# A graph layer's main path written out without loops, with 24 row buffers in turn, on one Trainium2 core

## The reference, cut to what matters

```python
h = jnp.maximum(_layernorm(x, axis=-1), 0.0)
hx = jnp.einsum('ni,rio->rno', h, weight)         # 8 x 12500 x 256
msg = hx[edge_type, src]
agg = jax.ops.segment_sum(msg, dst, num_segments=12500)
out = x + agg * 0.5 ** 0.5 + h_bias + (h @ loop_weight) * 0.5 ** 0.5
```

## Time and profile before

| what | value |
|---|---|
| median of 3 runs | 2342.75 us |
| the profiled execution, first to last instruction | 2975.6 us |
| instructions recorded | 39409 |
| first gather starts | 146.6 us |
| GpSimd's 1661 gathers, busy | 1631.7 us |
| TensorE busy (products of sums, of weights) | 1792.1 us (747.5, 1176.8) |
| VectorE busy | 1201.0 us |

### The profile page before, as it was taken

How to read it: one execution, slowest core, us unless ns; L and a number is a source line. 1 busy time by engine, 2 the same in 40 slices (tenths; PEclk the granted TensorE clock), 3 DMA queues, 4 the chain that set the end, 5 groups by cost and what they waited for, 6 DMA issues and landing times.

```text
span 2975.6 us, 39409 instructions
## 1 busy us (share of the span) xinstructions
PE 1792.1 (60%) x10566; PEld 1293.5 (43%) x10566; DVE 1201.0 (40%) x2675; ACT 520.9 (18%) x590; POOL 1699.8 (57%) x1687
## 2 busy tenths in 40 slices
PE   0046665665666666666675665666666665755667
PEld 0024444454444444444454444444444444443445
DVE  9834333343344343333343333333443334333433
ACT  4401111111111111111111111111111111111111
POOL 5466556565565565556555556466566555565553
PEclk9997777777777777777777767777777777777778
DMA  6533323333333333333333323233333333333232
GB/s 221 180 119 97 86 79 104 90 94 92 90 93 94 95 94 92 87 91 96 88 94 89 92 80 100 76 97 97 89 99 96 86 92 93 89 97 88 81 89 64
DMA packets 128701, 287.90 MB, mean 97 GB/s; under 512 B 31806, under 2 KB 71738, under 8 KB 125614
## 3 DMA queue, kind: packets, MB, share of 16 engines
q0 software_dynamic: 79728, 217.82, 26.0%
q1 hardware_dynamic: 47122, 57.12, 5.9%
q10 hardware_dynamic: 1836, 12.80, 1.0%
HBM read 262.01 MB, written 25.60 MB: 97 GB/s over the span
## 4 chain that ended last, share of the span: by engine, by line
PE 46%; issue 26%; DVE 12%; another core or an unknown queue 10%; DVEq 4%; DMA 1%; POOL 1%; ACT 0%; POOLq 0%; ACTq 0%; SPq 0%
PE ps_out L789 31%; PE sums L815 14%; DVE ring L683 4%; DVE onehot L641 2%; DVEq L672 2%; DVE result L662 1%; DVE stats L546 1%; DVE ring L652 1%; POOL rows L370 1%; PE ps_out L794 1%; DVEq L683 1%; DVE mv L563 1%; DMA rows<-h_table,index_now 1%; DMA xg<-x 0%
## 5 line engine op out<-in xcount | busy, mean ns | idle before, releaser
L370 POOL DMA_INDIRECT rows<-h_table,index_now x1661 | 1631.7, 982 | 1179.3 <-PE sums L815 531.0
L683 DVE TENSOR_TENSOR ring<-ring,sums 128x256 f32 x1661 | 700.3, 422 | 1715.5 <-remote 915.8
L789 PE MATMUL ps_out<-w_sb,stage 128*128 128x256 f32 x3072 | 1176.8, 503 | 208.7 <-issue 199.8
L815 PE MATMUL sums<-onehot,rows 128*128 128x128 f16 x6644 | 747.5, 245 | 869.5 <-issue 569.1
L815 PEld LDWEIGHTS sums<-onehot,rows 128*128 128x128 f16 x6644 | 526.0, 110 | 1189.6 <-issue 828.1
L789 PEld LDWEIGHTS ps_out<-w_sb,stage 128*128 128x128 f32 x3072 | 698.1, 250 | 378.0 <-issue 309.3
L452 ACT COPY index_now<-src_i 128x8 int32 (+1 forms) x196 | 38.8, 198 | 2128.0 <-PE sums L815 1687.0
L641 DVE TENSOR_TENSOR onehot<-lane,slot 128x768 f16<-128x768 f16 (+1 forms) x293 | 270.7, 924 | 0.4 <-issue 0.4
L459 ACT COPY stage<-ring 128x2048 f32 (+1 forms) x96 | 182.2, 1898 | 227.2 <-DVE carry L654 147.8
L462 ACT COPY ring<-zeros 128x2304 f32 (+1 forms) x96 | 202.8, 2112 | 10.9
L794 PE MATMUL ps_out<-w_sb,own_hT 128*128 128x256 f32 x384 | 112.6, 419 | 0.0
(11 more groups left out here) (52 smaller groups left out, 244.0 us busy)
## 6 DMA issues: line engine op xcount, KB each, us to landing
rows<-h_table,index_now POOLq DMA_INDIRECT x1661
own<-h_table SPq DMA_DIRECT2D x97, 128.0 KB
own_x<-x SPq DMA_DIRECT2D x97, 128.0 KB
out<-result SPq DMA_DIRECT2D x97, 128.0 KB
xg<-x SPq DMA_DIRECT2D x12, 1024.0 KB, 6.1
h_table<-tg ACTq DMA_DIRECT2D x12, 1024.0 KB, 8.2
w_sb<-weight SPq DMA_DIRECT2D x2, 1024.0 KB
dst_i<-dst SPq DMA_DIRECT2D x1, 833.0 KB, 10.5
```

The lines of the kernel that those rows point to most:

```text
L370: nc.gpsimd.indirect_dma_start(out=rows[:, k, :], out_offset=None, in_=table[:, :], in_offset=bass.IndirectOffsetOnAxis(ap=index_now[:, k: ...
L683: nc.vector.tensor_tensor(window, window, sum_of(k).rearrange("p (a w) -> p a w", w=W), ALU.add).then_inc(added, 1)
L789: nc.tensor.matmul(ps_out[:, 0:D], stage[:, m, :], w_sb[:, h, r, :], start=(m == 0), stop=False)
L815: last = nc.tensor.matmul(sum_of(k)[:, h * P:(h + 1) * P], rows[:, k, part * D + h * P:part * D + (h + 1) * P], onehot[:, k, :], start=(pa ...
```

## The change

All four compute engines and SP run the main path as straight code: every step, every wait value and every address is a constant. Further:
- GpSimd reads a chunk's indices from `src_i` itself; the copies by ScalarE and the waits on them are gone. `rows` has 24 buffers used in turn, with one wait for every four gathers.
- The ring is four tiles of 128 columns one behind the other and 16 columns behind the last. Only a window at the ring's end spills; `merge_spill` adds it to the ring's head and zeroes it once in four steps. `carry_tile` is gone. A window's offset is the node modulo 512, one VectorE piece in the head.
- `own`, `own_x` and `result` have two buffers each. `finish_tile` of a tile now comes after the second add of the next step.
- The 18 products of a tile are spread over the chunks from k = 5 on.
- The last two tiles are multiplied from the ring, with no copy, each in its own PSUM tensor; their own-row products go first.

```diff
-            def gather_step(s, count):
-                for k in range(count):
-                    for g, (a, b) in enumerate(INDEX_GROUPS):
-                        if k == a:
-                            pool.wait_ge(index_ready, len(INDEX_GROUPS) * s + g + 1)
-                    for a, b in BUFFER_GROUPS:
-                        if k == a:
-                            if not isinstance(s, int) or s > 0:
-                                pool.wait_ge(summed, K * (s - 1) + b)
-                            pass_gate(pool, pool_passed)
-                    nc.gpsimd.indirect_dma_start(
-                        out=rows[:, k, :], out_offset=None, in_=table[:, :],
-                        in_offset=bass.IndirectOffsetOnAxis(ap=index_now[:, k:k + 1], axis=0),
-                    ).then_inc(landed[k], 16)
+            def gather(c):
+                if c >= NB and c % NB_STEP == 0:
+                    pool.wait_ge(summed, c - NB + NB_STEP)
+                nc.gpsimd.indirect_dma_start(
+                    out=rows[:, c % NB, :], out_offset=None, in_=table[:, :],
+                    in_offset=bass.IndirectOffsetOnAxis(ap=src_i[:, c:c + 1], axis=0),
+                ).then_inc(landed[c % NB], 16)
...
-                gather_step(0, K)
-                with pool.Fori(1, STEPS - 1) as s:
-                    gather_step(s, K)
-                gather_step(STEPS - 1, K_LAST)
+                pool.wait_ge(s_src, 16)
+                for c in range(E_CHUNKS):
+                    gather(c)
...
             def stage_tile(t):
-                act.wait_ge(carried, t + 1)
+                act.wait_ge(added, chunks_before(t + 2))
+                if t % RING == 0:
+                    act.wait_ge(merged, spills_before(t + 1))
...
-                nc.vector.scalar_tensor_tensor(
-                    offsets[:, :, 0:K], tile_of.rearrange("p (s k) -> p s k", k=K), float(SLOT),
-                    within.rearrange("p (s k) -> p s k", k=K), ALU.mult, ALU.add).then_inc(s_window, 1)
+                nc.vector.tensor_scalar(offsets[:, :, 0:K], base_i[0:1, :].rearrange("p (s k) -> p s k", k=K),
+                                        SPAN - 1, None, ALU.bitwise_and).then_inc(s_offsets, 1)
...
-                nc.vector.tensor_tensor(head, head, carry[:, :, :], ALU.add).then_inc(spill_added, 1)
-                dve.wait_ge(spill_added, t + 1)
-                nc.vector.tensor_copy(carry[:, :, :], ring[:, :, bass.ds(ring_slot(t) + P, W)]
-                                      ).then_inc(carried, 1)
+            def merge_spill(t, count):
+                head, spilled = ring[:, :, 0:W], ring[:, :, SPAN:SPAN + W]
+                dve.wait_ge(added, count)
+                nc.vector.tensor_tensor(head, head, spilled, ALU.add).then_inc(merged, 1)
+                dve.wait_ge(merged, spills_before(t + 1))
+                nc.vector.memset(spilled, 0.0).then_inc(spill_cleared, 1)
+                dve.wait_ge(spill_cleared, spills_before(t + 1))
...
+            def last_own_product(i, h):
+                if h == 0:
+                    pe.wait_ge(hT_copied, TILES - 1 + i)
+                    pe.wait_ge(added, E_CHUNKS - NSUM + 1 + i)
+                nc.tensor.matmul(last_out[i][:, 0:D], last_hT[i][:, h, :], w_sb[:, h, R, :], start=(h == 0), stop=False)
+
+            def last_products(i):
+
+                t = TILES - 2 + i
+                pe.wait_ge(added, E_CHUNKS)
+                if t % RING == 0:
+                    pe.wait_ge(merged, spills_before(t + 1))
+                for m in range(HR):
+                    last = nc.tensor.matmul(last_out[i][:, 0:D], ring[:, m, ring_slot(t):ring_slot(t) + P],
+                                            w_sb[:, m // R, m % R, :], start=False, stop=(m == HR - 1))
+                last.then_inc(out_ready, 1)
...
-                    if k >= begin:
-                        now = 2 if len(products) > count - 2 - k else 1
-                        for m in products[:now]:
-                            tile_product(s - 2, m)
-                        products = products[now:]
+                    if k >= FIRST_PRODUCT:
+                        now = -(-todo // (count - k))
+                        for m in range(HR + H - todo, HR + H - todo + now):
+                            tile_product(s - 2, m)
+                        todo -= now
```

More of the change, by code:

```diff
@@ L148, in relational_graph_layer @@
         ahead_of = rows_room[:, 0:C].bitcast(i32)
[L149 to L154, removed]
+        last_hT = [xg[:, 2, i, :].rearrange("p (h n) -> p h n", h=H) for i in range(2)]
         NSUM = 6
@@ L159, in relational_graph_layer, with sum_of @@
         ps_hT = pb("ps_hT", [P, 512], fp32)
-        last_out = sums[0]
-        def sum_of(k):
-            return sums[k % NSUM][:, 0:HR * W]
+        last_out = [sums[(E_CHUNKS + i) % NSUM] for i in range(2)]
+        def sum_of(c):
+            return sums[c % NSUM][:, 0:HR * W]
         s_x = [sem(f"x_loaded{i}") for i in range(XB)]
@@ L222, in relational_graph_layer @@
         act_passed = sem("scalar_gates_passed")
-        stored = sem("result_stored")
+        stored = [sem(f"result_stored{b}") for b in range(2)]
         block = ctx.enter_context(nc.Block())
@@ L314, in general_tile, with general_x_tile, general_store @@
                              ).then_inc(g_tile, 16)
+                if not isinstance(t, int) or t > 0:
+                    sp.wait_ge(hT_ready, t)
+                sp.dma_start(own[0:n, 0, :], table[bass.ds(t * P, n), :]).then_inc(own_landed[0], 16)
+            def general_x_tile(t, n):
+                sp.dma_start(own_x[0:n, 0, :], x[bass.ds(t * P, n), :]).then_inc(x_landed[0], 16)
+            def general_store(t, n):
+                sp.wait_ge(result_ready, t + 1)
+                sp.dma_start(out[bass.ds(t * P, n), :], result[0:n, 0, :]).then_inc(stored[0], 16)
             sp.wait_ge(s_flag, 1)
@@ L664, in finish_tile @@
                 dve.wait_ge(scaled, t + 1)
-                nc.vector.tensor_tensor(result[0:n, :], result[0:n, :], bias_b[0:n, :], ALU.add
+                nc.vector.tensor_tensor(result[0:n, b, :], result[0:n, b, :], bias_b[0:n, :], ALU.add
                                         ).then_inc(result_ready, 1)
-            def vector_step(s, count, closes, finish, ahead, ahead_count=K):
+            def finish_tile(t, product=ps_out):
+                dve.wait_ge(x_landed[t % 2], 16 * (t // 2 + 1))
+                if t >= 2:
+                    dve.wait_ge(stored[t % 2], 16 * (t // 2))
+                scale_product(t, P if t < TILES - 1 else LAST, t % 2, product)
@@ L797, in tile_product, with tensor_step @@
                         last.then_inc(out_ready, 1)
-            def tensor_step(s, count, finish, begin=8):
-                products = list(range(HR + H)) if finish else []
+            def tile_product(t, m):
+                if m == 0:
+                    pe.wait_ge(staged, t + 1)
+                    if t > 0:
+                        pe.wait_ge(scaled, t)
+                product(t, m)
+            def tensor_step(s):
+                count = chunks_before(s + 1) - K * s
+                todo = HR + H if s >= 2 else 0
                 for k in range(count):
+                    c = K * s + k
                     for g, (a, b) in enumerate(ONEHOT_GROUPS):
@@ L851, in general_tile @@
                 last.then_inc(g_turned, 1)
-                whole_tile(t)
+                pe.wait_ge(own_landed[0], 16 * (t + 1))
+                if not isinstance(t, int) or t > 0:
+                    pe.wait_ge(hT_copied, t)
+                turn_rows(0)
+                pe.wait_ge(staged, t + 1)
+                if not isinstance(t, int) or t > 0:
+                    pe.wait_ge(scaled, t)
+                for m in range(HR + H):
+                    product(t, m)
             pe.wait_ge(s_unfit, 5)
```

311 lines of the change are left out of this document (128 added, 183 removed).

## The result

The changed kernel takes 2350.99 us (median of 5 runs, 2349.06 to 2353.4), the kernel before beside it 2342.3 us (5 runs): ratio 1.0042, 95% interval 1.0031 to 1.0053. It is slower by 0.42%, 8.7 us. The forecast was 2328; the sign was wrong. The rival "one-hots hit more gathers" had 2349. A ratio in this document is taken from each kernel's fast executions alone, so it can differ from the ratio of the medians beside it, for `unroll` above all.

A forecast was written before the change was run, and what follows sets the result against it. GpSimd's gather pace was taken as the bound: floor 2310.8 us, less 2.7 (head), 5.1 (carries) and 3.0 (tail), is 2300.0; with 31.9 - 4 = 27.9 above it, 2327.9, put as 2328 us. Range 2297 to 2358.

The forecast's parts named there:

- one-hots hit more gathers: Rival, 22%: products from the 6th chunk move VectorE's one-hots onto more GpSimd gathers, which then take longer; 2349 us.
- The bound: GpSimd's gather pace sets the plain run's time: 1.306 us per gather, against 1.287 in the lower limit worked out.
- the floor: Time at GpSimd's own pace without waits: head 146.6, gathers 1631.7, distances between them 505.2, tail 27.3; 2310.8 us.
- The reading of the 632.9 us: Profiled execution (2975.6 us) over the plain median (2342.75): most of GpSimd's waits there were taken as caused by the recording.
- the 31.9 us above the floor: Plain median less the floor: kept as the limit of what GpSimd's waits cost in plain runs; 27.9 us after the change.
- the carries: VectorE's ring: 98 carry adds go, 25 merges come, so fewer gathers are delayed at the port; 5.1 us of gain.
- Loops: Loops of GpSimd and the other engines written out: value 0, with 5 us of gain or loss as ends.
- Indices and buffers: GpSimd's index copies and waits go, 24 row buffers in turn: 4 us of gain, bounds 0 and 31.9.
- the waits were real: Rival, 15%: GpSimd's waits for indices make up all of the 31.9 us and all go; 2300 us.
- Head: Window offsets before the first gather: one VectorE piece stays of three; 2.7 us of gain, bounds 0 and 3.6.
- Tail: Last ring add to last product: no carries or copies, own products first; 3.0 us of gain, bounds 1.9 and 3.8.
- Products over 12 chunks: TensorE's 18 products of a tile spread over 12 chunks instead of 9: worth 0 under GpSimd's pace.

The follow-up runs named there:

- unroll: The kernel before with its four compute-engine loops written out: 3054.7 us (ratio 1.0112) and 3024.59 us (1.0148), where the kernel before took 2965.0 and 2981.15 us.
- after_l: The changed kernel with the sums' low halves left out, two matmuls per chunk in place of four: 2347.71 us, ratio 1.0031 to the kernel before.
- before_l: The kernel before with the sums' low halves left out, two matmuls per chunk in place of four: 2334.24 us, ratio 0.9965 to the kernel before.
- after_l_fp8_b: after_l with the products from k = 8 again, two per chunk: 2339.49 us, ratio 0.9992 to the kernel before (2341.54 us beside it).

## Why the prediction was wrong

**The bound** was right. GpSimd gathers without a real wait on an even chip, at the pace the floor used: the 1660 distances sum to 505.7 us (505.2 in the floor).

**The reading of the 632.9 us** was wrong in kind. I took them for the recording's. The profiled execution of the changed kernel is the lowest of its five (2349.06 us), that of after_l is the highest of its ten, 11 us over their median; nothing near 633 us. On uneven chips the plain runs of the kernel before take 2965 to 2981 us, which is the span of the profile. So the waits in the earlier trace rows are, by all that the runs show, real and of another chip. The conclusion, that they don't bear on the 2342.75 us, held.

**The step that failed** is the one on the port, and it failed twice. First the base: the earlier trace rows with a mean of 982 ns, 54.8 us above the median gather, come from a run in which GpSimd often stood still when a one-hot was made, so fewer gathers were there to be hit: one-hots lengthen 124 of them by 49 us. On an even chip before_l has 998 ns, and one-hots lengthen 207 by 83 us. With the prediction's head, distances and tail, the kernel before's 2341.3 us leave (2341.3 - 1.8 - 146.6 - 505.2 - 27.3) / 1661 = 1000 ns (1.8 us lie between a time and its span). That is an estimate, and it supposes that the kernel before has no real waits on an even chip, as before_l has none. By it 29 of the 31.9 us above the floor, which the prediction kept as waits of some kind and cut by 4 for indices and buffers, are one-hots at work. Second the change: the forecast let the one-hots stay as they were, and credited 5.1 us for the carries. Measured, the third one-hot costs 12 to 25 us more than in before_l, and the carry additions lengthen two gathers of before_l, by 0.4 us in all: they stand behind the third one-hot, 93 of the 98 in a gather that has already started. The bias addition now falls on the start of 23 to 44 gathers, 2 to 4 us. Of the 14.8 us of gain that were forecast, 9.1 (carries, indices and buffers) do not show, and the one-hots turned the rest into a loss.

**The rival** "one-hots hit more gathers" named the mechanism. It put the cause in the products that begin at the 6th chunk, and after_l_fp8_b bears that out. That its value (2349) is also the time is luck: it was half of 196 one-hots that always hit, counted from 982 ns, while only the third one-hot of a step moved for the worse, and the base was 1000. Its point of decision, a mean gather of 988 ns, was counted from 982; from 1000 it would have been 1006, just where the gathers are.

**Loops:** 0, right on an even chip: 506.0 us of distances in before_l with loops, 506.0 in after_l and 505.7 in the changed kernel without. The fetch per step, which the prediction derived and the back-edge did not show, does not exist either: the kernel before fetched 15 packets of code in its whole execution, by the queues of its profile. On uneven chips the loops were worth 1.1 to 1.5%, against writing them out. **Indices and buffers:** 4 us expected; before_l shows 0. Its products are lighter, though, and it is 7 us faster than the kernel before, of which no trace on an even chip exists. How much of the 7 us are waits of the full kernel stays open; "the waits were real" (2300 us) is out as a forecast, since the changed kernel has none and is slower. **Head:** 2.7 us expected, 146.6 - 144.2 = 2.4 measured. **Tail:** from the last ring addition to the end of the last product 15.2 us were expected. The timeline, as the earlier trace rows:

```profile
2327.80 0.42 DVE L636 TENSOR_TENSOR ring<-ring,sums 128x256 f32 x1 [0.72 <-PE sums L767]
```
```profile
2330.15 13.98 PE L730 MATMUL sums<-w_sb,ring 128*128 128x256 f32 x64
```

2344.13 - 2328.22 = 15.9 us, 3.1 us less than before: the 3.0 is right for this stretch. But from the last gather's end to the span's end it is 26.0 us for 27.3: 1.3 us of gain, for the last sum is added 6.9 us after the last gather now and was 5.2. And the 27.3 are an uneven chip's: in the pair of one even chip the tail is 26.6 us in before_l and 26.8 in after_l, so nothing of the 3.0 arrives there. **Products over 12 chunks:** put at 0, under GpSimd's pace. In the stand-ins they cost some 9 us, not by their own duration but by the moment that they give to a one-hot.

The sum of the terms against the 2339.5 us span worked out for the kernel before: head -2.4, gathers 1671.4 - 1660.4 = +11.0, distances +0.5, tail -1.3: +7.8, and the span is 2347.3. It closes by construction, for the 1660.4 are what the other terms leave. The profiled pair before_l and after_l, where every term is measured, goes the same way: gathers +22.2, distances 0, head -2.2, tail +0.2, +20.3 us in all (13.5 by the medians).

**Left open:** why some chips are uneven. It is not the fetching of straight code alone: the looped kernel does it too, which fetches 15 packets of code (the changed one 162). And the changed kernel itself was not run on such a chip, only its near forms.

## What to carry to other kernels

Where one engine's pace is the bound, price every edit of another engine also by the moment at which it makes that one's instructions fall: here a step judged "hidden" moved a one-hot by 0.3 us and, in the stand-ins, cost some 9 us, against 14.8 us of savings forecast and less measured. A mean in a profile is good for the execution it is from only: hold the profiled execution's time against the plain runs, and when they disagree take no duration that depends on overlap from it. And when two engines share a port, take one operand off it rather than tune the order: that gained 4% on an even chip, ten times the 0.4% lost by the change. On the uneven chips, where GpSimd's pace was not the bound, the same edit to the kernel before, with one sum buffer less, cost 3.3%.

## What the runs showed of the hardware

- A gather (indirect DMA of 128 rows issued by GpSimd) that starts under a VectorE instruction with two SBUF inputs is longer by the overlap less 0.13 us: in the seven cases worked out from rows here (0.12 to 0.60 us more), and in all of the 210 gathers that one-hots lengthen in the changed kernel. One that starts within 0.04 us of the one-hot's start is not lengthened (14 cases), and none of the 377 that start under an instruction with one input in PSUM. With one of the inputs in PSUM nothing is added (947 ns mean), and the VectorE instruction is no slower (906 against 927 ns on the mean for the one-hots, all forms).
- One and the same kernel takes 2341 us on some chips and 2965 to 2981 us on others. On those TensorE stands still for 0.7 us or a multiple between matmuls that wait for nothing, and in the kernel before some register instructions of VectorE and SP, in their loops, take 0.7 us (41 and 37).
- 162 packets of straight code in place of 15 put no gap between gathers on an even chip (505.7 and 506.0 us).
